# GpSimd's residual sum behind the norm, the first expert's scaling in the wait for the power, and a narrower wait before the second expert's GELUs

## The reference

```python
x = x + attn_block(layernorm(x))
x = x + moe_block(layernorm(x))
```

```python
kv = einsum('bhnd,bhne->bnde', fk, v);  qkv = einsum('bhnd,bnde->bhne', fq, kv)
attn = qkv / (einsum('bhnd,bnd->bhn', fq, fk.sum(1))[..., None] + 1e-6)
x = q_x + attn @ wo + bo
h = gelu(layernorm(x) @ fc_w + fc_b);  return x + h @ proj_w + proj_b
```

## Time and profile before

| | |
|---|---|
| median of 3 runs | 1291.31 us (1289.68 to 1294.83) |
| the profiled execution | 1284.61 us, its span 1282.8 us |
| mean granted TensorE clock | 0.896 of full speed |
| busy: TensorE matmul | 1075.2 us, 84% |
| busy: TensorE weight load (beside the matmuls) | 795.2 us, 62% |
| busy: VectorE | 798.2 us, 62% |
| busy: ScalarE | 526.7 us, 41% |
| busy: GpSimd | 186.4 us, 15% |
| DMA | 170.17 MB, mean 133 GB/s |

### The profile page before, as it was taken

One profiled execution on the slowest core, in us unless ns is written; L12 is line 12 of the kernel. 1 busy time (PEld: TensorE's weight loads), 2 busy tenths in 40 slices (PEclk: granted clock), 3 DMA queues, 4 the chain that ended last, 5 costly groups with the idle time before them and its releaser, 6 DMA issues.

```text
span 1282.8 us, 21648 instructions
## 1 busy us (share of the span) xinstructions
PE 1075.2 (84%) x7112; PEld 795.2 (62%) x7112; DVE 798.2 (62%) x1692; ACT 526.7 (41%) x835; POOL 186.4 (15%) x113
## 2 busy tenths in 40 slices
PE   5655978889797989899997989899898988795947
PEld 3343857667575758485765758476766667583723
DVE  2555666666666676766666676766666674655333
ACT  2313443536353454545362444535362443141422
POOL 1011202020202112121201112121203011111000
PEclk9758998979797989899897989999898989797979
DMA  4985747472838474656747374655747385211113
GB/s 166 179 160 140 132 132 156 116 171 91 179 90 179 126 172 126 148 122 163 156 138 165 109 173 115 151 128 156 163 131 179 117 173 127 70 50 33 42 66 114
DMA packets 242516, 170.17 MB, mean 133 GB/s; under 512 B 177040, under 2 KB 218256, under 8 KB 240144
## 3 DMA queue, kind: packets, MB, share of 16 engines
q1 hardware_dynamic: 235792, 158.80, 52.6%
q10 hardware_dynamic: 6656, 10.50, 2.3%
HBM read 93.75 MB, written 75.50 MB: 132 GB/s over the span
## 4 chain that ended last, share of the span: by engine, by line
issue 57%; PE 22%; DVE 10%; POOL 6%; ACT 3%; DMA 1%; DVEq 1%; ACTq 1%; POOLq 0%; SPq 0%
PE pq L963 7%; PE ps L926 3%; PE pj L949 3%; POOL rs L448 2%; PE pq L871 2%; PE pt L935 2%; DVE am L701 2%; PE pj L1052 2%; DVE acc L819 1%; DVE stat L622 1%; DVE hn L632 1%; POOL rs L459 1%; ACT hidden L542 1%; POOL x L452 1%; PE pt L859 1%
## 5 line engine op out<-in xcount | busy, mean ns | idle before, releaser
L717 DVE TENSOR_TENSOR hidden<-xhT,hidden 128x512 fp32r<-128x512 f32 x128 | 104.3, 815 | 227.2 <-ACT hidden L542 227.0
L541 ACT ACTIVATE xhT<-pq,col 128x512 f32<-128x512 f32 x128 | 88.1, 688 | 345.7 <-PE pq L963 345.5
L963 PE MATMUL pq<-hT,w_fc 128*128 128x512 f32 x768 | 223.3, 430 | 5.6 <-issue 4.3
L949 PE MATMUL pj<-w_pj,hidden 128*128 128x256 f32 x1536 | 214.0, 288 | 2.7 <-DVE hidden L717 2.7
L949 PEld LDWEIGHTS pj<-w_pj,hidden 128*128 128x128 f32 x1536 | 191.3, 189 | 17.3 <-DVE hidden L717 3.7
L926 PE MATMUL ps<-kq 48*128 48x128 f32 x1024 | 155.3, 434 | 38.3 <-DVE am L701 22.8
L926 PEld LDWEIGHTS ps<-kq 48*128 48x128 f32 x1024 | 133.8, 329 | 78.9 <-issue 42.6
L701 DVE TENSOR_TENSOR am<-ps,mask 128x512 f32<-128x512 f32 x256 | 164.1, 682 | 18.3 <-PE ps L926 14.6
L963 PEld LDWEIGHTS pq<-hT,w_fc 128*128 128x128 f32 x768 | 148.9, 207 | 35.9 <-issue 5.2
L871 PE MATMUL pq<-zT,w_e 128*128 (+1 forms) x256 | 116.1, 602 | 9.6 <-DMA b_e<-in_eb 7.2
L459 POOL TENSOR_TENSOR rs<-var,mhalf 128x4 f32<-128x4 f32 x16 | 16.2, 1010 | 559.4 <-DVE var L745 559.4
(11 more groups left out here) (114 smaller groups left out, 1334.4 us busy)
## 6 DMA issues: line engine op xcount, KB each, us to landing
kq<-scratch_q SPq DMA_DIRECT2D x192, 128.0 KB, 3.6
kq<-scratch_k SPq DMA_DIRECT2D x192, 128.0 KB, 4.5
scratch_q<-hidden SPq DMA_DIRECT2D x32, 512.0 KB, 4.6
scratch_k<-hidden SPq DMA_DIRECT2D x32, 512.0 KB, 6.1
scratch_nd<-ot SPq DMA_DIRECT2D x16, 1024.0 KB, 3.9
nd<-scratch_nd SPq DMA_DIRECT2D x48, 256.0 KB, 3.4
x_sb<-in_x SPq DMA_DIRECT2D x16, 512.0 KB, 5.1
scratch_v<-feat_v ACTq DMA_DIRECT2D x16, 512.0 KB, 2.8
```

The costliest lines, as they stand in the source:

```text
L541: nc.scalar.activation(gelub[:, u], pq[u][:, :], ACT.Gelu, bias=b_fc[:, m:m + 1])
L717: nc.vector.tensor_tensor(hidden[:, m % SLOTS, 1], gelub[:, u], hidden[:, m % SLOTS, 0].bitcast(f32), ALU.subtract).then_inc(S["rest_ready ...
L949: last = nc.tensor.matmul(pj[u][:, D * s:D * (s + 1)], hidden[:, m % SLOTS, a, lo:lo + P], w_pj[:, b, m], start=(m == 0 and n == 0 and s = ...
L963: last = nc.tensor.matmul(pq[m % 2][:, :], w_fc[:, b, c, P * m:P * (m + 1)], hT[:, a, c], start=(n == 0), stop=(n == len(order) - 1))
```

## The change

Three edits.

1. GpSimd's residual sum (L464) moves from stage A2 to stage R and waits for h_ready, the end of the norm of R, where it waited for the two additions into x1. s_ready is now raised in R.
2. F1 and R change places in both lists. TensorE and ScalarE have no part in R, so only VectorE's queue changes: the two scaling instructions of F1 stand ahead of the four of the norm. On GpSimd the power stays in A2.
3. ScalarE's GELUs of F3 wait for a count of acc_ready that is lower by 2, the count before F1's scaling: the last tile's sum (F4).

```diff
@@ FULL and HEAD, both lists alike
-        "R", "F1", "F3", "B0", "H", "F4", "FX", "B9", "F2"]
+        "F1", "R", "F3", "B0", "H", "F4", "FX", "B9", "F2"]
@@ INC
-    "y_ready": {"Y": 1}, "yb_ready": {"Y": 1}, "s_ready": {"P": 1, "A2": 1},
+    "y_ready": {"Y": 1}, "yb_ready": {"Y": 1}, "s_ready": {"P": 1, "R": 1},
@@ GpSimd
                 if p.stage == "A2":
-                    slot = x_sb[:, p.t % XRING]
                     wait("var_ready", at("var_ready", 1))
                     nc.gpsimd.tensor_tensor(rs[:, :], var2[:, 0], mhalf[:, 0:SUB], ALU.pow).then_inc(S["rstd_ready"], 1)
-                    for b in range(2):
-                        wait(f"ps_free{b}", at(f"ps_free{b}", 1))
+                if p.stage == "R":
+                    slot = x_sb[:, p.t % XRING]
+                    wait("h_ready", at("h_ready", 1))
                     wait("pool_chain", at("pool_chain"))
                     pool.sem_inc(held, 1)
                     nc.gpsimd.tensor_tensor(slot, slot, x1[:, :, :], ALU.add).then_inc(S["s_ready"], 1)
@@ ScalarE, stages F1 and F3
                     wait("chosen_in", at("chosen_in"))
-                    wait("acc_ready", at("acc_ready"))
+                    wait("acc_ready", at("acc_ready", -NC * e))
```

## The result

The changed kernel takes 1250.64 us (median of 4 runs, 1242.56 to 1253.45) against 1290.49 (4 runs) for the kernel before: ratio 0.9677, 95% interval 0.9625 to 0.9729. The forecast was 1254, range 1237 to 1270. The medians differ by 39.9 us, the profiled executions, 1284.61 and 1249.88, by 34.7; the sum of the steps was 36.6.

The account below looks back on a forecast made before the run. Bound by VectorE's queue between variance and expert sum, by TensorE elsewhere. Savings per pass, 19.2 + 3.6 + 3.6 + 10.2 = 36.6 us, off the median of 1291.3 gave 1254.7, predicted as 1254; range 1237 to 1270.

Parts of the forecast that it names:

- The norm is held by the sum: VectorE's norm, one instruction in four held 2.04 us beside GpSimd's residual sum; moving the sum saves 2.0 per pass.
- The sum beside the masks costs 0: GpSimd's moved sum runs beside VectorE's masks, one operand from PSUM; collision taken as 0, other end a full 2.35 us.
- The scaling hides in the wait for the power: VectorE's two scalings, 0.86 us, fit its 1.12 us wait for GpSimd's power; power 0.1 longer, swallowed by 0.3 slack.
- Rival 2: GpSimd and VectorE exclude each other for whole instructions, power too: norm starts at P+1.8, 2.4 us given back, 1257; 8%.
- Second experts' GELUs: On ScalarE they wait only for their matmuls (P+1.6), are done at P+2.3, ahead of the h copies.
- TensorE's own order is next: Scores B0 then limit the masks (P+2.75); L963, first up-projection matmul, starts at P+8.5, 3.2 us saved on pass 12.
- It passes on: After L963 TensorE is the bound until the next pass, so the time saved before it shortens the whole.
- Rivals 3 and 5: Sum blocks VectorE's masks, 1278 us, 4%; q and k loads or numerators' round trip take half back, 1273 us, 7%.
- rival 4: VectorE's norm, now queued behind the expert's GELUs and scaling, is delayed when GELUs end late; near 1297 us; 2%.
- The clock: TensorE's granted clock still falls in the stretch before L963: 0 taken, 24 us possible gain, some 5 possible loss.
- rival 1: With gaps of 1.6 us at most, TensorE's clock stays up on most passes: up to 24 us more, 1231; 12%.

Follow-up runs that it names:

- Changed: The kernel with all three edits, against the kernel before: 1250.64 us, ratio 0.9677; 1248.49 us, ratio 0.9698, when measured again.
- the change with fill: The changed kernel plus three unread 128x512 matmuls ahead of B9's scores and three behind, passes 7 to 16: 1231.18 us, ratio 0.9571 to the kernel before.

## Why the prediction was right

*The norm is held by the sum.* Right, to the size: 2.01 saved on each of passes 2 to 6 (2.04 foreseen), longest norm 416 ns.

*The sum beside the masks costs 0.* Right: the masks take 1.29 beside it and 1.27 before, the sum 2.39 instead of 2.35. This step was the one that mattered most, and I had not seen how much. What follows the norm on VectorE here takes one operand from PSUM. The two experiments without edit 2 put the scaling there, which works from SBUF to SBUF, and there the whole 2.1 us comes back. A third instruction in the kept traces narrows it down. L717 has the masks' operation and size, but both its operands lie in SBUF, and early in many of the following passes it meets another addition of GpSimd. After pass 12 of the changed kernel:

```profile
823.08 2.39 POOL L455 TENSOR_TENSOR x_sb<-x_sb,row 128x1024 f32 x1
824.19 1.83 DVE L717 TENSOR_TENSOR hidden<-xhT,hidden 128x512 fp32r<-128x512 f32 x1 [2.13 <-ACT hidden L542]
827.37 1.08 PE L935 MATMUL pt<-am,vb 128*32 128x128 f32 x32 [0.46 <-DVE am L701]
```

Over that trace, 15 of the 128 L717 start while a GpSimd instruction of 128x1024 runs, and all 15 are held, 873 to 2032 ns against a median of 691; of the masks 50 do, and none is over 692 ns. The third line shows what is still to be had: the masks behind L717 are late, and TensorE idles 0.46 us for them. The margin on the other side was thin. F4's sum, with both operands in SBUF, starts at P+5.37, and GpSimd's sum ends at P+5.28, where I had 5.2 and 4.85.

The prediction's sum was right because it followed the changed order instruction by instruction; I went wrong as soon as I priced the edits one at a time.

*The scaling hides in the wait for the power.* Right; the power takes 1.26 beside it, not 1.1. The norm starts at P+1.30, 0.26 late, and ends at P+2.68, still ahead of the end of B0's scores (P+2.74). The slack that I gave, 0.3, took it up.

*Rival 2, whole instructions exclude each other.* Its first half came true: the first scaling holds the power. Where that scaling starts 0.09 before the power (passes 8 to 10 and 12 to 14) the power takes 1.26, where it starts 0.14 before (7 and 11) 1.20, and on pass 16 of the second measurement of Changed, where it starts 0.03 after the power, 1.02. The earlier the scaling is over, the less the power is delayed, by the same 0.05. Its second half did not: the rival had the norm at P+1.8 and the scalings at 0.43 + 1.01 + 0.43; they took 0.88 together, so the power holds nothing. The Trainium skill (SBUF, Who interferes with whom) states an exclusive lock, held for the whole instruction by whoever issues first. For the sum of 128x1024 the runs agree (a norm or scaling behind it waits for its end: 2446, 2603 ns); for a power of 128x4 they do not, since the second scaling beside it is not held. The page also says that a VectorE instruction with at most one input in SBUF, outside the two-port modes, does not contend, and the masks agree.

*Second experts' GELUs.* Done at P+2.3 as foreseen. That the wait's removal by itself brings nothing here was left unsaid in the prediction and is shown by the kernel without edit 3.

*TensorE's own order is next.* Right: masks at P+2.77 on passes 8 to 10 and 12 to 14 and at P+4.0 on 7 and 11 (2.75 and 4.1 foreseen), L963 at P+8.67 (8.5) and P+9.7 (9.8). Pass 10 I had wrong: its L963 was never at P+11.7 but at P+16.29, behind the gap at the loop's end, and is now at P+12.46. It saved 3.8 where I had 3.2, so the error did not show in the sum. The 0.17 is there already where the h subtractions start (P+4.16 for 4.0), a step between engines of 0.1 to 0.2 that I had not counted.

*It passes on.* Right, 34.0 of 34.6. Rivals 3 and 5 did not happen; of rival 4 only its harmless part did. On passes 16 and 17 the norm did wait for the experts' scaling (P+1.70 and 1.85), the mechanism of rival 4, hidden as expected on 16 by B0.

*The clock.* The term was 0, and in the two profiled executions it came out near 0: F2 takes 1.96 or 1.97 on all 11 passes, before and after, and the mean granted clock went from 0.896 to 0.901. Over more runs it is less clear. The kernel before has 0.886 to 0.898 in the runs of the experiments, Changed 0.901 to 0.914, and the four runs of the first measurement go from 1253.45 us at 0.902 to 1242.56 at 0.914. So part of the 3.3 us by which the medians' difference (39.9) exceeds my 36.6 may be the clock, a small part of rival 1; no run separates it. The reason I gave for 0 does not hold as I gave it. I expected the fall because the work between the gaps stays short matmuls; with wide matmuls in the gaps the clock stays up, though the short ones stay as they are. The gaps of 0.4 and 1.5 us that the change leaves, with only that work between them, were still enough for a fall. Rival 1 put up to 24 us on a clock that stays up; the change alone does not get them, the change with fill gets 17.

## What to carry to other kernels

Moving an operation out of the way of another need not remove a collision, it may only pick the next victim: look at what stands behind it on the other engine and where its operands lie. Here an SBUF-to-SBUF scaling was held for 2.1 us, and masks with one operand in PSUM were not held at all. Edits of one path are to be priced together, along the new order; priced apart they gave 12.7 and 14.4, together 40. And a gap on TensorE can cost more behind it than in it: wide matmuls thrown away in gaps of 0.4 and 1.5 us gave 17 us.

## What the runs showed of the hardware that I had not expected

The hold goes to whichever instruction that works in SBUF alone meets GpSimd's sum: the norm (2446 ns), the scaling (2594 to 2603 ns), or, where the sum starts ahead of it, the second scaling (2.10 us). A power of 128x4 on GpSimd is itself held by a scaling that started before it (1.26 us instead of 1.01), and holds none (0.88 us for two). TensorE's clock fell in a stretch where its gaps were 0.4 and 1.5 us with narrow matmuls between them, and stayed up when six matmuls of 128x512 (0.97 us for three) were put around B9's scores.
